# Residual of the down projection summed by Pool and DVE, half a chunk each

## The reference

```python
x = x + jnp.tanh(g_xattn[0]) * _L0_xattn_ref(_layernorm(x), ctx_1024, ctx_1024, ...)
x = x + jnp.tanh(g_ffn[0]) * _L0_ffn_ref(_layernorm(x), ...)

def _L0_ffn_ref(x, clip_x, clip_down, w_gate, w_up, w_down):
    xq = _act_fake_quant(x, clip_x[0])
    gate = jnp.einsum('bsh,ih->bsi', xq, _weight_fake_quant(w_gate))
    up = jnp.einsum('bsh,ih->bsi', xq, _weight_fake_quant(w_up))
    h = _act_fake_quant(jax.nn.silu(gate) * up, clip_down[0])
    return jnp.einsum('bsi,hi->bsh', h, _weight_fake_quant(w_down))
```

## Time and profile before

| | |
|---|---|
| median of 3 runs | 588.55 us (588.35 to 588.63) |
| profiled execution | 589.7 us |
| its span, first to last instruction | 587.8 us |
| busy in the span | PE 564.7 us, DVE 531.4 us, ACT 444.8 us, POOL 241.1 us |
| mean granted clock of TensorE | 0.999 of full speed |

### The profile page before, as it was taken

The page is one execution under the profiler, slowest core; times in us unless marked ns, Lnnn a source line. Parts: engine busy times, 40 slices in busy tenths (PEclk is TensorE's granted clock), DMA queues, the critical chain, the costliest instruction groups (busy, mean ns, idle before and its releaser), DMA issues. The chain is left out here.

```text
span 587.8 us, 18041 instructions
## 1 busy us (share of the span) xinstructions
PE 564.7 (96%) x6579; PEld 265.2 (45%) x6584; DVE 531.4 (90%) x684; ACT 444.8 (76%) x874; POOL 241.1 (41%) x366
## 2 busy tenths in 40 slices
PE   9999999999999999999999999999999999999985
PEld 4555655234344444444444444444444533544364
DVE  3999999999999999999899899899899885699988
ACT  2667776267787897897897897798799673799694
POOL 2799999701310335453224214215214211366400
PEclk9999999999999999999999999999999999999999
DMA  8579864422212222221231122122121000000024
GB/s 272 186 239 349 286 221 158 135 89 91 69 60 77 79 65 56 76 84 54 59 100 58 54 84 78 54 70 92 55 56 55 3 2 1 2 1 1 1 108 178
DMA packets 29902, 55.21 MB, mean 94 GB/s; under 512 B 5544, under 2 KB 19752, under 8 KB 29864
## 3 DMA queue, kind: packets, MB, share of 16 engines
q1 hardware_dynamic: 29864, 54.71, 29.0%
HBM read 37.62 MB, written 16.78 MB: 93 GB/s over the span
## 5 line engine op out<-in xcount | busy, mean ns | idle before, releaser
L929 ACT ACTIVATE prob<-st_ps 128x512 f32<-128x512 f32 x512 | 280.7, 596 | 61.6 <-PE st_ps L787 54.4
L787 PE MATMUL st_ps<-q,k 98*32 98x512 bf16 x2048 | 178.3, 380 | 1.9 <-ACT prob L929 1.9
L989 DVE TENSOR_REDUCE negm<-xT_ps 128x2 f32<-128x1024 f32 x128 | 154.5, 1207 | 7.3 <-PE xT_ps L339 6.8
L989 DVE TENSOR_REDUCE negm<-v_ps 128x2 f32<-128x1024 f32 x128 | 154.3, 1205 | 3.8 <-PE v_ps L339 3.8
L811 PE MATMUL pv_ps<-prob,v_u 128*32 128x512 f32 x1024 | 132.5, 592 | 0.6 <-ACT prob L929 0.3
L787 PEld LDWEIGHTS st_ps<-q,k 98*32 98x32 bf16 x2048 | 57.0, 95 | 90.8 <-ACT prob L929 34.0
L1181 POOL TENSOR_TENSOR msplit<-negm,onesf 128x16 bf16<-128x16 f32 x32 | 7.1, 221 | 205.8 <-DVE negm L989 205.8
L339 PE MATMUL xT_ps<-k,q 96*32 96x512 bf16 x1024 | 78.4, 379 | 1.1 <-DVE negm L989 1.0
L339 PE MATMUL v_ps<-k,q 96*32 96x512 bf16 x1024 | 78.1, 380 | 1.3 <-DVE negm L989 0.9
L339 PEld LDWEIGHTS xT_ps<-k,q 96*32 96x32 bf16 x1024 | 27.0, 96 | 36.6 <-issue 12.9
L811 PEld LDWEIGHTS pv_ps<-prob,v_u 128*32 128x32 f32 x1024 | 31.1, 110 | 26.8 <-issue 2.8
(11 more groups left out here) (149 smaller groups left out, 786.5 us busy)
## 6 DMA issues: line engine op xcount, KB each, us to landing
qk_parts<-parts SPq DMA_DIRECT2D x32, 384.0 KB, 3.2
k<-qk_parts SPq DMA_DIRECT2D x32, 192.0 KB
q<-qk_parts SPq DMA_DIRECT2D x32, 192.0 KB
ctx<-in_ctxT SPq DMA_DIRECT2D x8, 512.0 KB, 4.7
X<-in_x SPq DMA_DIRECT2D x8, 512.0 KB, 6.4
k<-qk_parts SPq DMA_DIRECT2D x32, 128.0 KB
q<-qk_parts SPq DMA_DIRECT2D x32, 128.0 KB
out<-X SPq DMA_DIRECT2D x7, 512.0 KB, 2.6
```

What stands on the lines that cost most here:

```text
L787: last = nc.tensor.matmul(score_bank(i)[lo:lo + COLS, :], k6[g][:, h, kt * P + lo:kt * P + lo + COLS], q6[g][:, h, :], start=True, stop=True)
L929: nc.scalar.activation(prob[kt % 2][:, h, :], score_bank(HPU * kt + h)[:], ACT.Exp, scale=SCALE).then_inc(exp_done, 1)
L989: nc.vector.tensor_reduce(negm[g % 2][:, lo:lo + 2], pair[:], op=ALU.max, axis=AX.X, negate=True).then_inc(mx_read, 1)
```

## The change

The residual of every chunk is split in halves of two tiles, 512 values per partition. DVE sums the first half and POOL the second; of the last chunk POOL sums the first and DVE the second. Each engine has its own semaphore (`sum_dve`, `sum_pool`), and SP waits for both before the store of a chunk. For the last chunk each of the two stores waits for one of them. `scale_out` of chunk n waits for POOL's sum of chunk n - 2, since it writes over the same `y1` buffer. POOL's eight sums stand behind its 24 products of the third stage.

```diff
+        def residual(eng, ns, n, t0, done, summed):
+
+            eng.wait_ge(y1_ready, done)
+            x = X[:, 4 * n + t0:4 * n + t0 + 2, :]
+            ns.tensor_tensor(x, y1[n % 2][:, t0:t0 + 2, :], x, ALU.add).then_inc(summed, 1)
...
                 def scale_out(n, t0, t1):
 
                     dve.wait_ge(y_ready, 2 * n + t1 // 2)
+                    if n >= 2:
+                        dve.wait_ge(sum_pool, n - 1)
...
-                def residual(n, t0, t1, done):
-
-                    dve.wait_ge(y1_ready, done)
-                    x = X[:, 4 * n + t0:4 * n + t1, :]
-                    nc.vector.tensor_tensor(x, y1[n % 2][:, t0:t1, :], x, ALU.add).then_inc(out_ready, 1)
...
                     if n:
-                        residual(n - 1, 0, 4, n)
+                        residual(dve, nc.vector, n - 1, 0, n, sum_dve)
                 for i in range(2):
                     scale_out(NCH - 1, 2 * i, 2 * i + 2)
-                for i in range(2):
-                    residual(NCH - 1, 2 * i, 2 * i + 2, NCH + i)
+                residual(dve, nc.vector, NCH - 1, 2, NCH + 1, sum_dve)
...
+                for n in range(NCH):
+                    residual(pool, nc.gpsimd, n, 2 if n < NCH - 1 else 0, n + 1, sum_pool)
...
                 for n in range(NCH - 1):
-                    send(4 * n, 4 * n + 4, n + 1)
-                for i in range(2):
-                    send(4 * (NCH - 1) + 2 * i, 4 * (NCH - 1) + 2 * i + 2, NCH + i)
+                    sp.wait_ge(sum_dve, n + 1)
+                    sp.wait_ge(sum_pool, n + 1)
+                    send(4 * n, 4 * n + 4)
+                sp.wait_ge(sum_pool, NCH)
+                send(4 * NCH - 4, 4 * NCH - 2)
+                sp.wait_ge(sum_dve, NCH)
+                send(4 * NCH - 2, 4 * NCH)
```

More of the change, by code:

```diff
@@ L1339, in build @@
         y1_ready = sem("y1_ready")
-        out_ready = sem("out_ready")
+        sum_dve = sem("sum_dve")
+        sum_pool = sem("sum_pool")
         out_done = sem("out_done")
@@ L1648, in _, with send @@
                 out_v = out_dram
-                def send(t0, t1, ready):
-                    sp.wait_ge(out_ready, ready)
+                def send(t0, t1):
                     sp.dma_start(out_v[:, t0:t1, :], X[:, t0:t1, :]).then_inc(out_done, DMA)
                 for n in range(NCH - 1):
-                    send(4 * n, 4 * n + 4, n + 1)
-                for i in range(2):
-                    send(4 * (NCH - 1) + 2 * i, 4 * (NCH - 1) + 2 * i + 2, NCH + i)
+                    sp.wait_ge(sum_dve, n + 1)
[5 more added lines that the diff above has]
+                send(4 * NCH - 2, 4 * NCH)
                 sp.wait_ge(out_done, (NCH + 1) * DMA)
```

## The result

The changed kernel takes 592.59 us, median of 5 runs (592.05 to 593.22), against 588.63 us before (588.35 to 589.35) in the same comparison: a ratio of 1.0063, 95% interval 1.0051 to 1.0074. It is slower by 3.96 us. The forecast was 592.5. The medians further down leave out two far slower runs, one of 728.93 us (half of the residual left out) and one of 3320.31 us (the fills).

What follows compares the result with a forecast made beforehand. DVE was taken to bound the down projection. Seven chunks at 1.08 lost less 0.54 saved gave +3.8 us, the last chunk 0.1: +3.9, profiled 593.6, less 1.15 for the median, 592.5 us; range 589.2 to 594.8.

Steps and rivals of the forecast that it cites:

- DVE sets the pace: Down projection: DVE has no idle time up to its last sum and a chunk costs it 3.27 or 3.14 us.
- the half saves 0.54 us a chunk: Moving half the residual off DVE saves 1.135 - 0.595 = 0.54 us per chunk, 3.8 us in seven chunks.
- a waiting POOL goes before DVE's next instruction: Chunks 0 to 6: POOL's sum gets in behind DVE's clip, and DVE's residual half then has to wait for it.
- the rival of half and half: POOL gets in only in about four chunks and hides beside scale_out in the others: +0.6, 589.2 us; chance 0.06.
- 1.08 us a stand: DVE's loss each time its instruction is held by POOL's 1.27 us sum: 1.08 us, bounds 0 and 1.42.
- The handover: From DVE's instruction to POOL's waiting one: POOL's work begins 0.08 us before the start of DVE's next.
- the rival of the slow handover: POOL begins its sum 0.27 us later after DVE's clip: +5.8 us, 594.3 us; chance 0.05.
- The sum: Per chunk 1.08 - 0.54 = +0.54 us, +3.8 in seven chunks, last chunk 0.1 later: total +3.9 us.
- Costed at nothing: Priced at zero: scale_out's second wait, SP's two waits, and the clips being late for PE and ACT.
- The rival with the clock: PE's gaps grow to about 1.4 us and its clock falls to half: +3.7 us, 596.2 us; chance 0.03.
- The race in the narrow chunks: Narrow-clip chunks: POOL's sum and DVE's half arrive almost together; if DVE goes first, the clips wait instead, same price.
- the rival in which POOL hides beside the scale: POOL stays out until the next scale_out and holds up nothing: -2.8 us, 585.7 us; chance 0.15.

Runs made afterwards that it cites:

- the fills: Kernel before plus seven POOL fills of 128 x 1280 f32 that read nothing, released by each scale_out: 589.54 us, ratio 1.0022.
- the spare sums: Kernel before, whole residual on DVE, plus seven POOL sums of 128 x 512 f32 whose result nothing reads: 596.36 us against 588.64, ratio 1.0134.

## Why the prediction was right

- **DVE sets the pace, and the half saves 0.54 us a chunk.** Right. In the run with the half left out DVE's narrow residual costs 0.60 from start to start (579.65 to 580.25), 0.54 below the whole one's 1.14.
- **The residual half stands for POOL's sum, and a waiting POOL goes before DVE's next instruction.** Right, and this decided the sign. It was read from a first-stage row of 0.65 us for a tiny POOL operation; the spare sums showed it for whole sums of POOL, with no wait of DVE added, 7.7 us for seven. POOL's sum held DVE in all seven chunks of the changed kernel, so the rival of half and half falls.
- **1.08 us a stand.** Right: 1.76 - 0.68 = 1.08 in the changed kernel, the 0.68 being the one half that did not stand. The handover was as read too: POOL's work began at 580.25 + 1.39 - 1.27 = 580.37, and DVE's clip ends at 580.50 by its row. From one `scale_out` to the next it is 3.81 us (578.96 to 582.77), and 3.69 from residual to residual (580.42 to 584.11); the forecast was 3.75. The Trainium skill (SBUF — State Buffer, "A bandwidth-pool intuition that's wrong (but worth ruling out)") gives the end of DVE's operation plus about 115 ns, measured where GpSimd writes DMA descriptors. By that POOL would have begun at about 580.6, an estimate; the trace has 580.37 and does not agree with that figure for a POOL sum, so the rival of the slow handover falls.
- **`scale_out` is free of POOL.** Right. With POOL's sum beside it, it took 1.22 us, as without.
- **The sum.** +3.8 for the chunks, +0.1 for the last one; 3.88 and 0.08 measured.
- **Costed at nothing:** the waits on `sum_pool` and of SP, PE and ACT. Right; the spare sums put no wait on DVE or ahead of a store and cost what they should. The rival with the clock falls: PE's gaps grew to 1.44 us, its 28 matmuls still took 2.90 us, and the mean granted clock of the execution was 0.998.
- **The race in the narrow chunks.** I left open who wins. POOL did in all three such chunks of the changed kernel; with the spare sums, and with the last chunk on DVE, DVE won once in three, with the same 0.04 us between them. The price was the same (clips of 1.82 in place of 0.75 us), as forecast.
- **What was off.** ACT's waits for DVE were put at some 5 us and are 3.2. Seven long residual rows were forecast and six came, since in the first chunk the clips stood. Instructions that follow each other on DVE overlap by 0.10 to 0.11 us in the earlier trace rows, not by 0.08; the costs were read from start to start, so nothing hangs on it. And the rival in which POOL hides beside the scale was priced too well: -2.8 us, since I let the last scale follow ACT's end by 1.0 us. Its place in the working is "then the last clip 0.2, four matmuls 0.4 and about 0.4 of handovers"; the last clip stood behind a whole `scale_out`, 1.69 us in all, and with the half left out the runs showed -2.3. With 1.69 in place of 1.0 the rival's own sum comes to -2.2.

That rival described a real version all the same. POOL did not stay out until the next `scale_out` by itself in any of the seven chunks; with a later release the code keeps it out.

## What to carry to other kernels

Work given to POOL is not free because POOL is idle. Where DVE's next instruction is a sum of two SBUF operands or an int16 clip like the ones here, DVE stood for nearly the whole of POOL's sum (1.08 of 1.27 us), and the half that left DVE saved it only 0.54. Put such a POOL operation beside a DVE instruction that reads PSUM and is about as long, by choosing the semaphore that releases it. To see who goes first, look in the trace for a short POOL operation among DVE sums. When the bound engine is relieved, read what comes next at the end of the stage before the gain is priced: of the 3.8 us freed on DVE here, ACT and the last clip behind a whole scale took 1.5 even with no sum on POOL; with POOL's sums beside the scale, one clip that stood took 0.3 more, and a last store that had become late 0.5.

## What was not expected of the hardware

- A fill of POOL (1.25 us, no reads) did not hold DVE's sum of two SBUF operands (1.21 us), as expected, but it held an int16 to bf16 clip for 1.05 us, which was not.
- With 0.04 us between the two issues the order was not always that of the issues: POOL's row starts at 569.33 and DVE's at 569.37, and DVE went first, as at 569.44 and 569.48 with the last chunk on DVE; at 584.07 and 584.11 in the changed kernel POOL did. What decides such a near tie is left open.
